# Two cross-attention layers on one core: where the values of a head pair land in PSUM, how far behind the square sums follow, and in what order the stages stand

## The reference, cut to what matters

```
layer 0:  q = x Wq;  k, v = ctx_text Wk, ctx_text Wv          (20 heads of 8)
          p = softmax(q k / sqrt 8) over the 60 text tokens
          text = p v
          qsem = l2norm(p ctx_text)                            (256 wide, per head)
          fused = q k_ip / sqrt 8 + 0.5 * qsem . l2norm(ctx_ip)   (4 prompt tokens)
          ip = softmax(fused) * spatial_mask, times v_ip
          x = (text + ip) W_out + b_out + x
layer 1:  x = softmax(q k / sqrt 8) v Wo + bo + x              (64 text tokens, no prompt part)
```

## Time and profile before

| what | value |
|---|---|
| runs | 486.33, 493.0 and 489.53 us; median 489.53 |
| the profiled execution | 493.66 us, its span 490.8 us |
| PE busy | 459.4 us (94%) |
| DVE, ACT, POOL busy | 301.1, 228.4, 172.4 us (61%, 47%, 35%) |
| TensorE clock, mean share granted | 0.959 |
| instructions | 13296 |

### The profile page before, as it was taken

How to read it: one execution, slowest core, us unless ns; L and a number is a source line. 1 busy time by engine, 2 the same in 40 slices (tenths; PEclk the granted TensorE clock), 3 DMA queues, 4 the chain that set the end, 5 groups by cost and what they waited for, 6 DMA issues and landing times.

```text
span 490.8 us, 13296 instructions
## 1 busy us (share of the span) xinstructions
PE 459.4 (94%) x5116; PEld 259.4 (53%) x5116; DVE 301.1 (61%) x858; ACT 228.4 (47%) x511; POOL 172.4 (35%) x345
## 2 busy tenths in 40 slices
PE   8876898999999999999999998988999999999896
PEld 4332454555555555555555555545566556655553
DVE  2131555786768677767866785655567657766553
ACT  2432233444444444443445444454556655755461
POOL 0621313535443543536356245353223313311000
PEclk9895978999999999999999999988999999999898
DMA  8698602503406217026034160160625726548211
GB/s 210 93 145 168 84 1 44 85 3 57 70 3 100 27 33 95 3 44 84 4 69 56 38 88 4 38 88 21 106 66 60 114 48 91 93 80 143 85 30 40
DMA packets 26281, 33.28 MB, mean 68 GB/s; under 512 B 4552, under 2 KB 17548, under 8 KB 26060
## 3 DMA queue, kind: packets, MB, share of 16 engines
q1 hardware_dynamic: 24268, 30.74, 38.3%
q10 hardware_dynamic: 1952, 1.70, 1.5%
HBM read 5.56 MB, written 2.62 MB: 17 GB/s over the span
## 4 chain that ended last, share of the span: by engine, by line
PE 89%; DMA 4%; DVE 3%; issue 2%; ACT 1%; DVEq 0%
PE ps L418 29%; PE ps L557 18%; PE ps L516 9%; PE ps L490 8%; PE ps L630 7%; PE ps L591 5%; PE ps L642 3%; DMA qs<-mt 3%; PE ps L563 3%; PE ps L532 2%; PE ps L611 2%; PE ps L501 1%; PE ps L607 1%; DVE mx L848 1%; DMA ca<-in_ctxT 1%
## 5 line engine op out<-in xcount | busy, mean ns | idle before, releaser
L745 ACT ACTIVATE pt<-ps 128x512 f32<-128x512 f32 x160 | 92.0, 595 | 37.8 <-PE ps L516 36.3
L848 DVE TENSOR_REDUCE mx<-ps 128x8 f32<-128x480 f32 (+3 forms) x192 | 105.6, 578 | 6.2 <-PE ps L490 6.2
L563 PE MATMUL ps<-pt,vb 64*32 64x256 f32 x640 | 108.0, 393 | 0.0
L557 PE MATMUL ps<-pt,gram 64*32 64x256 f32 x1280 | 102.1, 393 | 3.1 <-DVE mx L848 0.7
L532 PE MATMUL ps<-wt,cst 64*32 64x256 f32 x640 | 91.9, 388 | 0.0
L337 POOL TENSOR_TENSOR qp<-qr,qp 80x512 bf16<-80x512 f32 x32 | 37.0, 1156 | 127.8 <-ACT qp L730 127.8
L809 DVE TENSOR_TENSOR qr<-ps,qp 80x512 f32<-80x512 f32 x32 | 22.0, 686 | 83.9 <-ACT qp L726 83.9
L817 DVE TENSOR_TENSOR wt<-ps,pt 128x512 f32<-128x512 f32 x80 | 55.0, 687 | 23.3 <-PE ps L557 23.1
L516 PE MATMUL ps<-qs,ks 101*128 101x256 bf16 x320 | 61.5, 283 | 5.3 <-DMA qs<-mt 5.0
L418 PE MATMUL ps<-x,wq 80*80 80x512 f32 x128 | 64.1, 625 | 1.4 <-DVE qr L809 1.4
L490 PE MATMUL ps<-ks,qs 96*128 96x128 bf16 x640 | 58.4, 222 | 5.5 <-issue 2.3
(11 more groups left out here) (91 smaller groups left out, 623.0 us busy)
## 6 DMA issues: line engine op xcount, KB each, us to landing
qs<-qp SPq DMA_DIRECT2D x96, 160.0 KB, 4.6
ks<-kp SPq DMA_DIRECT2D x96, 80.0 KB, 3.6
out_T<-x SPq DMA_DIRECT2D x16, 160.0 KB, 5.0
x<-in_xT SPq DMA_DIRECT2D x1, 1920.0 KB, 12.5
ca<-in_ctxT ACTq DMA_DIRECT2D x2, 512.0 KB, 7.0
x<-in_xT SPq DMA_DIRECT2D x2, 320.0 KB, 8.2
qs<-mt ACTq DMA_DIRECT2D x32, 20.0 KB
wk<-in_WK SPq DMA_DIRECT2D x2, 160.0 KB, 5.0
```

The source lines that it names most:

```text
L557: last = nc.tensor.matmul(ps[T * hh + 32 * m:T * hh + 32 * m + 32, bank, sub * S:(sub + 1) * S], gram[keys_of(hh), r, 32 * m:32 * m + 32], ...
L563: nc.tensor.matmul(region(c, hh), vb[0][keys_of(hh), r, pair, :], pt[keys_of(hh), r, pair, :], start=(sub == 0 and c in (0, 1, 4)), stop=F ...
L745: nc.scalar.activation(pt[:, g % 2, 2 * c:2 * c + 2, :].rearrange("p a b -> p (a b)"), ps[:, 2 + (g + c) % 2, :], ACT.Exp, scale=SCALE).th ...
L848: nc.vector.tensor_reduce(mx[:, tile, p0:p0 + np_, :], o[:, :, :, 0:nt], AX_X, ALU.max).then_inc(red_done, 1)
```

## The change

Four things are changed.

**Places.** The pairs of a chunk no longer share a column quarter: the quarter follows the pair's parity. `GROUPS` puts chunks 0 and 1 in the first group, 2 alone in the second, 3 and 4 in the third (bank 7). `vb[0]` gets a new layout with 80 columns a chunk, so that a pair's weights are still 32 adjacent columns. The order of heads in `wo0` and `wrem` follows, loaded with 17 late DMAs in place of 13, and POOL's scaling of the prompt scores in `ipb` is cut from one instruction of 160 columns into ten of 16.

**Square sums.** They follow three pairs later in place of two, and each of them waits for its own w; `rd` itself no longer does.

**Transposes.** `mt` takes 80 columns as weights (the tail is zeros or the other tile's maxima) in place of 40, so it stands at partition 0 of a bank of its own (bank 0, in layer 1 bank 4), where it stood in quarters 2 and 3 of bank 7. In `ot` the group with 64 rows now has 128, and one of its three products is an ordinary fp32 product with 64 columns of the identity.

**Offsets.** All five tables are new. From one `st` 0 to the next in layer 0, PE: st0, sc0 (+1), st1, vw (-2), rd0, sc1, rd1, st2, sc2, sc3, st3, rd2, sc4, ot0 (-1), st4, rd3, ot1 (-1), rd4, mt (+1), zt, q, y, vk. ACT: exp0, ipe, exp1, qm, otev2, exp2, exp3, stat 0 (-1), stat 1 (-1), exp4, mtev, rsq, the DMA of the maxima, ztev, qh, otev1, gram. DVE: red4, on 0, neg, w3, on 1, ipa, w4, qr, ysb, vprep, ipm. In layer 1 `mt` now stands ahead of ot1 and pv2 ahead of vk. The output stores on SP move from 11.571 to 24.571.

```diff
+GROUPS = ((0, 1), (2,), (3, 4))
+GROUP_SLOT = (0, 8, 12)
...
-    ("st", 4): (0.489, 0.404), ("rd", 3): (0.574, None), ("rd", 4): (0.681, None), ("q4", 0): (0.851, None),
-    ("ot", 0): (1.553, 1.383), ("ot", 1): (1.596, 1.638), ("vw", 0): (1.957, None), ("zt", 0): (2.702, 2.191),
+    ("rd", 3): (0.565, None), ("rd", 4): (0.609, None), ("q4", 0): (0.891, None), ("ot", 0): (1.522, 1.391),
+    ("ot", 1): (1.587, 1.739), ("vw", 0): (1.935, None), ("zt", 0): (2.652, 2.283), ("y", 0): (2.804, 2.783),
...
-    ("exp", 2): (0.216, 0.054), ("exp", 3): (0.27, 0.081), ("exp", 4): (0.324, 0.432),
-    ("otev1", 0): (0.838, 0.676), ("otev2", 0): (1.162, 0.757), ("stat", 0): (1.297, None),
-    ("stat", 1): (1.351, None), ("rsq", 0): (1.595, None), ("ipe", 0): (1.919, None), ("ztev", 0): (2.622, 2.405)}
+    ("exp", 2): (0.297, 0.108), ("exp", 3): (0.351, 0.216), ("exp", 4): (0.486, 0.703),
+    ("otev1", 0): (0.784, 0.865), ("otev2", 0): (1.27, 0.973), ("stat", 0): (1.432, None),
+    ("stat", 1): (1.459, None), ("rsq", 0): (1.568, None), ("ipe", 0): (1.946, None), ("ztev", 0): (2.622, 2.189)}
...
-    ("outd", 0): (None, 11.571)}
+    ("outd", 0): (None, 24.571)}
...
-                    last = nc.tensor.matmul(ps[MT0:MT0 + 4 * PAIRS, bank, tile * 128:(tile + 1) * 128],
-                                            mc[:, tile].rearrange("p a b c -> p (a b c)"), id16[:, :], start=True, stop=True)
+                    last = nc.tensor.matmul(ps[0:8 * PAIRS, bank, tile * 128:(tile + 1) * 128],
+                                            mc[:, tile:tile + 2].rearrange("p t a b c -> p (t a b c)"), id16[:, :],
+                                            start=True, stop=True)
...
-            def region(c, hh):
-
-                quarter, grp = (c % 2 + 2 * (1 - hh), c // 2) if c < 4 else (1 - hh, 2)
+            def region(pair, hh):
+
+                quarter, grp = pair % 2 + 2 * (1 - hh), place(pair // 2)[0]
...
+            def quad(g, pair, sem_=None):
+
+                chunk = pair // 2
+                sub = place(chunk)[1]
+                pe.wait_ge(w_done, 5 * g + chunk + 1)
...
-                need(pe, w_done, 5 * g + c)
...
-                    if c:
-                        quad(g, c - 1, sub, out6_ps if (c, sub) == (4, 1) else None)
+                    if pair >= QUAD_LAG:
+                        quad(g, pair - QUAD_LAG, out6_ps if pair - QUAD_LAG == 5 else None)
                     elif g:
-                        quad(g - 1, 4, sub, core_done if sub else None)
+                        quad(g - 1, pair - QUAD_LAG + PAIRS, core_done if pair + 1 == QUAD_LAG else None)
...
-                    p = 64 if grp == 2 else 128
-                    last = nc.tensor.transpose(ps[:, bank, grp * 128:grp * 128 + p],
-                                               ots[0:p, grp, tile * 128:(tile + 1) * 128], cst[0:p, C_ID:C_ID + p])
+                    rows = ots[:, grp, tile * 128:(tile + 1) * 128]
...
+                            last = nc.tensor.matmul(out, rows, firsts, start=True, stop=True)
...
+                            last = nc.tensor.matmul(ps[:, bank, 256:320], rows, ident[:, 0:64], start=True, stop=True)
...
-                nc.gpsimd.tensor_scalar(e160[:, 1, :, :], raw, SCALE, None, ALU.mult)
+                for chunk in range(HP):
+                    raw = ipraw[:, g % 4, :, 4 * chunk:4 * chunk + 4, :].rearrange("p t (s h) n -> p t h s n", h=2)
+                    own = scaled[:, :, slots_of(chunk), :].rearrange("p t (h s) n -> p t h s n", h=2)
+                    for tile in range(2):
+                        nc.gpsimd.tensor_scalar(own[:, tile], raw[:, tile], SCALE, None, ALU.mult)
```

More of the change, by code:

```diff
@@ L41, with place, slots_of, slot_heads @@
     [0, 128, 2, 2, 2, 2 * VW_COLS, 2 * H, 128]).tolist()
[L44 to L52, removed]
+GROUPS = ((0, 1), (2,), (3, 4))
+GROUP_SLOT = (0, 8, 12)
+def place(chunk):
+    grp = min(g for g in range(3) if chunk in GROUPS[g])
+    return grp, GROUPS[grp].index(chunk)
+def slots_of(chunk):
+    grp, sub = place(chunk)
+    step = len(GROUPS[grp])
+    return slice(GROUP_SLOT[grp] + sub, GROUP_SLOT[grp] + sub + 3 * step + 1, step)
+def slot_heads():
+    heads = [0] * H
+    for chunk in range(HP):
+        for quarter, slot in enumerate(range(H)[slots_of(chunk)]):
+            heads[slot] = 2 * (2 * chunk + quarter % 2) + 1 - quarter // 2
+    return heads
+HEADS0 = slot_heads()
 def constants():
@@ L142, in sequence, with quadrants @@
     return [f[1:] for f in sorted(at)]
-def quadrants(what, k):
-    if (what, k) == ("pv", 2):
+def quadrants(what, g, k):
+    if (what, k) == ("pv", 2) and g >= B:
         return (0, 1)
-    return {"mt": (2, 3), "q": (0, 1, 2), "y": (0, 1, 2)}.get(what, (0, 1, 2, 3))
+    return {"mt": (0, 1, 2), "q": (0, 1, 2), "y": (0, 1, 2)}.get(what, (0, 1, 2, 3))
 def bank_users():
@@ L163, in bank_users @@
         for name, n, bank in users:
-            places = [(bank, quadrant) for quadrant in quadrants(name, n)]
+            places = [(bank, quadrant) for quadrant in quadrants(name, g, n)]
             plan[name, g, n] = bank, sorted({last[p] for p in places if p in last})
@@ L213, in xattn_kernel @@
         wt = sb("wt", [128, 2, PAIRS, S])
-        vb = [sb(f"vb{n}", [128, 2, PAIRS, VW_COLS]) for n in range(2)]
+        vb = [sb("vb0", [128, 2, SLOT + HP * CHUNK_COLS]), sb("vb1", [128, 2, PAIRS, VW_COLS])]
         gram = sb("gram", [128, 2, T])
@@ L260, in by_chunk @@
         def by_chunk(ap):
[L262 removed]
+            chunks = ap[:, SLOT:].rearrange("p (j c) -> p j c", c=CHUNK_COLS)
+            return chunks[:, :, 0:2 * VW_COLS].rearrange("p j (b c) -> p j b c", c=VW_COLS)
         def consumed(f):
@@ L562, in rd @@
                     for hh in range(2):
-                        nc.tensor.matmul(region(c, hh), vb[0][keys_of(hh), r, pair, :], pt[keys_of(hh), r, pair, :],
-                                         start=(sub == 0 and c in (0, 1, 4)), stop=False, skip_group_check=True)
-                    if c:
-                        quad(g, c - 1, sub, out6_ps if (c, sub) == (4, 1) else None)
+                        nc.tensor.matmul(region(pair, hh), vb[0][keys_of(hh), r, v0 + VW_COLS * sub:v0 + VW_COLS * (sub + 1)],
+                                         pt[keys_of(hh), r, pair, :],
+                                         start=(c in (0, 3)), stop=False, skip_group_check=True)
+                    if pair >= QUAD_LAG:
+                        quad(g, pair - QUAD_LAG, out6_ps if pair - QUAD_LAG == 5 else None)
                     elif g:
-                        quad(g - 1, 4, sub, core_done if sub else None)
+                        quad(g - 1, pair - QUAD_LAG + PAIRS, core_done if pair + 1 == QUAD_LAG else None)
             def q4(g, _):
-                pe.wait_ge(w_done, 5 * g + 5)
-                for sub in range(2):
-                    quad(g, 4, sub, core_done if sub else None)
+                for pair in range(PAIRS - QUAD_LAG, PAIRS):
+                    quad(g, pair, core_done if pair == PAIRS - 1 else None)
             def out_of(pair):
@@ L628, in ot @@
                 for grp in range(3):
-                    p = 64 if grp == 2 else 128
-                    last = nc.tensor.transpose(ps[:, bank, grp * 128:grp * 128 + p],
-                                               ots[0:p, grp, tile * 128:(tile + 1) * 128], cst[0:p, C_ID:C_ID + p])
+                    rows = ots[:, grp, tile * 128:(tile + 1) * 128]
+                    if g // B == 0:
+                        out = ps[:, bank, GROUP_SLOT[grp] * SLOT:(GROUP_SLOT[grp] + 4 * len(GROUPS[grp])) * SLOT]
+                        if grp == 1:
+                            firsts = ident.rearrange("p (q c) -> p q c", c=VW_COLS)[:, :, 0:SLOT]
+                            last = nc.tensor.matmul(out, rows, firsts, start=True, stop=True)
+                        else:
+                            last = nc.tensor.transpose(out, rows, ident)
+                    else:
+                        if grp == 2:
+                            last = nc.tensor.matmul(ps[:, bank, 256:320], rows, ident[:, 0:64], start=True, stop=True)
+                        else:
+                            last = nc.tensor.transpose(ps[:, bank, grp * 128:(grp + 1) * 128], rows, ident)
                 last.then_inc(ot_ps, 1)
@@ L786, in _ @@
             nc.vector.memset(wt[:, 0, 0:2, :], 0.0).then_inc(wt_zeroed, 1)
-            for n in range(2):
-                nc.vector.memset(vb[n][:, :, :, :], 0.0).then_inc(zeroed, 1)
+            nc.vector.memset(vb[0][:, :, :], 0.0).then_inc(zeroed, 1)
+            nc.vector.memset(vb[1][:, :, :, :], 0.0).then_inc(zeroed, 1)
             nc.vector.memset(vpb[:, :, :, 0:IP_ROW], 0.0).then_inc(zeroed, 1)
+            nc.vector.memset(mc[:, 2, :, :, :], 0.0).then_inc(zeroed, 1)
             dve.wait_ge(c_in[0], 32)
```

76 lines of the change are left out of this document (42 added, 34 removed), and 24 rows, old and new, of tables (DVE_AT, FILL_BANK, PE_AT).

## The result

| | before | after |
|---|---|---|
| runs, us | 486.33, 489.53, 489.93, 493.0 | 475.28, 475.37, 475.78, 476.55 |
| median, us | 489.73 | 475.57 |
| profiled execution / its span, us | 493.66 / 490.8 | 476.55 / 474.8 |
| TensorE clock, mean share granted | 0.959 | 0.962 |

The ratio after/before is 0.9715, 95% interval 0.9647 to 0.9783: 14 us faster. The forecast was 484 (469 to 497), so the time lies in the range, but on the faster side and just outside the 476 to 492 that the prediction gave its own case. Executions of before differ more than those of after: in the runs made beside the experiments, executions of before with a mean granted clock of 0.974 or 0.975 have spans of 483.4 to 485.1 us, where the profiled one has 490.8 at 0.959.

The account below looks back on a forecast made before the run. PE was taken as the bound (89% of the chain of waits). Layer 0 -4.7, layer 1 -2.8, ends +2 gave -5.5 us, -1.1%, so 484 us as a median, range 469 to 497.

Parts of the forecast that it names:

- its own case: The likeliest case: new waits take back most of the saved PE work; 476 to 492 us, chance 0.63.
- Chunks 0 and 4: PE, layer 0: with pairs spread over eight tiles both cost what chunk 2 does, 0.85 and 0.82 us less per group.
- Wait for exp4: PE ahead of chunk 4 waits for ACT's exponential, now behind the second statistics copy: +1.0 us per group, bounds 0.8 and 1.2.
- The first rival: The wait for exp4 costs little, so the saved work arrives: 468 to 475 us as a median, chance 0.2.
- Transposes: PE, output tile 1 and maxima in fewer tile shapes: 0.20 us saved per group; at output tile 0 +0.06.
- q behind the maxima: PE's q waits for the copy of the maxima, both now in bank 0: +0.3 us per group, bounds 0 and 0.45.
- Square sums of pair 3: PE's first square sums wait for w of chunk 0: +0.15 us per group, up to 0.5 if DVE is late.
- POOL's ten scalings: POOL, prompt scores: 2.15 us in all, +1.5, hidden by the wait of 1.0; without it 0.3 to 0.5 cost.
- The second rival: The clock falls between ot1 and q: 503 us if every group, 492 if every third; chance 0.15, 0.11 over 2% slower.
- Stores: End of the kernel: all 16 output stores queue on SP and delay a DMA of the maxima, +2 us, bounds 0 and +4.
- Start: Four more late loads on SP, begun some 3 us earlier: 0 us, bounds -3 and +3.
- chunks 0 and 4 staying long: Rival: the change doesn't do what it says, as by the bank rule; +1.67 per group, 504 us, chance 0.02.

Follow-up runs that it names:

- e4: The changed kernel with the column quarters of head 0 and head 1 exchanged, so values and square sums share tiles with U; 535.48 us.
- e1: The changed kernel with the exponential of chunk 4 ahead of ACT's first statistics copy again; 467.47 us, 0.956 of before.
- e6: The kernel before with all five offset tables of the changed one, places, lag and transposes as before; 502.47 us, ratio 1.029.
- e2: The changed kernel with POOL's ten scalings put back to one of 160 columns, leaving out the reordering of the prompt scores; 472.31 us.
- e3: The changed kernel with chunk 4's exponential ahead of ACT's first statistics copy and one POOL scaling of 160 columns, reordering left out; 461.96 us.
- e5: The changed kernel with all five offset tables of the kernel before; 519.04 us, ratio 1.060.
- e9: As e12, and the output stores queued where the kernel before had them; 455.29 us.
- e12: The changed kernel with exp4 before ACT's statistics copies, setup copies before a cast, POOL's scalings before its waits, chunk 3's product before the negated maxima; 455.33 us.
- e8: The changed kernel with the output stores' offset as before (11.571 in place of 24.571); 479.67 us.

## Why the prediction was right in direction and too small in size

**Chunks 0 and 4** (-0.85, -0.82): right, 1.03 each. e4 shows the cause to be the shared tile. (The prediction's counts of 16, 8 and 8 products are records of the trace, two for each fp32 product of `rd`.) By the Trainium skill (TensorEngine Tiling (Array Packing), Gotcha 1: PSUM Pressure) different row tiles cannot access the same bank simultaneously; the trace does not agree, since values of both row halves go to one bank in the chunks of 1.03 as in those of 1.86.

**Wait for exp4** (+1.0): right in place and size, 0.85 idle and 0.91 of time in e1. e6 has the same wait. The first rival, that the wait costs little, is wrong; its time of 468 to 475 is about what e1 has with the wait taken away, 467.5. So part of the range that the result came near, below 476, was there for a reason that did not hold; that 475.57 lies in the range is in part luck.

**Transposes** (-0.20, +0.06): `ot` 1 without its wait and `mt` take 0.54 + 0.14 = 0.68 against 0.90, -0.22. The stretch with output tile 0 and one st and sc takes 199.35 to 200.30, 0.95, against 0.97: -0.02, not +0.06.

**q behind the maxima** (+0.3): too high. `zt` to `q` is 0.61 against 0.49, +0.13 in the median of the groups; `q` starts 0.76 behind `mt`, not 0.91.

**Square sums of pair 3** (+0.15): +0.35, because of the failed sub-step below. **Chunk 2** (+0.05): -0.04.

**POOL's ten scalings, "hidden by the very wait of 1.0"**: this step failed. They took the 2.16 us forecast (2.15), but `ipb` began 205.07 - 201.32 = 3.75 behind `ot` 1, not 3.11. The 3.11 was read from a timeline in which `mt` stood ahead of chunk 4. On ACT rsq stands behind the copy of the maxima, and `mt` had been moved behind chunk 4, so the wait for exp4 delays the chain as well as the thing that was to hide it. In e1, without the wait, `ipb` begins 3.10 behind `ot` 1 (217.56 - 214.46), but the next `st` 0 comes earlier too. e2 and e3 price the ten scalings at 0.31 a group either way.

**The sum's missing term**: from `st` 0 to chunk 0 is 194.50 - 192.85 = 1.65 against 201.15 - 199.28 = 1.87, -0.22, with `st` 1 ahead of `vw`. I moved that step in the list and never costed it. It comes with the order: e6, with the old places and the new order, has 1.65 as well. The stretch from `q` to the next `st` 0 was taken as unchanged and is 208.84 - 204.57 = 4.27 against 4.21, +0.06.

Sum by these rows: -0.85 - 0.82 - 0.22 - 0.02 + 0.91 + 0.13 + 0.35 - 0.04 - 0.22 + 0.06 = -0.72, measured -0.70, forecast -0.31. Over 15 groups the forecast was -4.7; measured -12.9, of which 10.5 is 15 times 0.70 and most of the rest comes from the second and third interval (17.59 to 15.87, 18.31 to 17.03), in which the clock fell in both kernels (before for 6.8 us from 61.0 and 3.4 from 81.5, after for 3.4 from 63.1 and 3.4 from 80.2).

**The change of layer** was costed at nothing and gave -4.0. Before, a stretch of 3.40 with PE busy 2.33 was followed by 6.9 us at 0.51. After, by stretch (length, PE, PEld, DVE, ACT, POOL, clock, DMA share, GB/s), with the first group of the middle of each layer:
```profile
200.00:220.00 20.00, 18.10 (x311) 10.23 (x309) 15.47 (x53) 8.19 (x21) 11.65 (x33) 1.00 0.41 78
400.00:420.00 20.00, 19.86 (x184) 12.57 (x181) 14.31 (x36) 13.19 (x26) 5.77 (x6) 1.00 0.50 78
...
311.90:315.30 3.40, 1.94 (x23) 1.57 (x16) 2.13 (x10) 1.43 (x6) 0.00 (x0) 1.00 0.17 20
315.30:322.20 6.90, 6.01 (x40) 3.32 (x39) 2.73 (x8) 3.80 (x11) 5.79 (x19) 1.00 0.02 5
```
PE was busy only 1.94 of 3.40 at the same place, and the clock stayed at 1.00. Half of 6.9 us is 3.4; the interval with it gave 2.8 (15.92 to 13.12), because PE's waits in it are longer than before (1.47 and 0.87 us in place of 1.07 and 0.51). The interval ahead of it gave 1.3, the one behind it -0.1. The second rival, the clock, did not come true in after: PE had 0.85 idle in every group, 18.10 busy of 20, and from 84 to 438 us no fall, and one fall that before had is gone. It did come true in e5, whose waits are 2.05 and 0.95, in six of twelve groups, and at the price of 1.55 us for a fall, where the prediction had 1.7. Whether the fall at the change of layer goes away by the change or by how the waits happened to lie was not settled. No other run shows before's 15.92 for that interval: with the new places theirs are 13.0 to 13.8, and e6, with the old places, has 14.7 with 3.4 us at 0.50 in it. But before was profiled in one execution only, and its executions differ in their mean clock.

**Layer 1** (-0.2 a group): 9.78 to 9.54, -0.24, right. **Stores** (+2): nothing, by e9 and e12. The wait for the DMA of the maxima near the end is 2.28 after and was 1.82 before; in the profiled execution the clock fell to 0.50 behind it for 6.8 us (438.6 to 445.4), and the next interval is 10.94. In e1, with the same 2.28, it fell for 3.4 us and the interval is 9.56. **Start** (0, -3 to +3): +2.2 in the profiled pair. ACT's setup copies had been moved behind a cast that waits for the third queries, and that queue I had not walked; PE waits 1.86 us for them. But the first `st` of kernels with this order lies between 44.8 and 48.6 us (52.3 in e8), so the cause of the +2.2 stays open.

**Two sums of the rivals** don't come out. A fall in every group is 25 us, and on the forecast of 484 that is 509, not 503; chunks 0 and 4 staying long is 15 times 1.67, 25 us, and gives 509 too, not 504. Neither changes a chance.

## What to carry to other kernels

Price a change of places and a change of order together: here each alone is slower and both together are faster. When an instruction is moved in one engine's list, follow every chain that starts behind it, and measure a cover from the event that releases it, not from the old distance: a wait that is to hide a chain may delay the chain too. When a kernel is much slower than its waits explain, look at the granted clock group by group, as in e5. Work that needs nothing from the wait it stands behind belongs ahead of it; four moves within the lists brought 475.6 to 455.3, more than the change itself.

## What the runs showed of the hardware that was not expected

- Where U and the values or square sums fall in the same 64x32 tiles, a chunk takes 1.86 us in place of 1.03, in all five chunks of e4, though they write to different banks; in different tiles, both row halves write values to one bank without any cost that shows.
- One tile with two products of a pair made a chunk as long (1.85, before's chunk 4) as four such tiles did (1.86, e4).
- A stretch in which PE was busy 2.33 of 3.40 us preceded a fall of the clock to 0.51, and one with 1.94 of 3.40 at the same place of the program did not; in e5 one with 1.55 did and one with 1.46 did not. Idle PE in a short stretch alone did not tell here when the clock falls.
- Ten scalings of 16 columns took 2.16 us on POOL, one of 160 columns 0.61.
